# A decoder layer on one Trainium2 core: two weight matrices centred once, two of the four norms without a mean, every engine's order written anew

## What is computed

```python
def _layernorm(x, axis=-1, eps=1e-05):
    m = jnp.mean(x, axis=axis, keepdims=True)
    v = jnp.var(x, axis=axis, keepdims=True)
    return (x - m) / jnp.sqrt(v + eps)
...
x = _layernorm(x + _L0_attn_ref(x, Wq, bq, Wk, bk, Wv, bv, Wo, bo, gamma, beta))
x = _layernorm(x + _L0_xattn_ref(x, ctx_1024, Wq, Wk, Wv, Wo))     # ... return out @ Wo
x = _layernorm(x + _L0_ffn_ref(x, w_gate, w_up, w_down))           # ... fp4_linear(h, w_down)
```

## Time and profile before

| | us |
|---|---|
| time, median of 3 runs | 372.71 (372.67 to 373.03) |
| span of the profiled execution (first to last instruction) | 371.1 |
| PE busy (matmuls, ends modelled) | 349.7 (94%) |
| DVE busy | 308.7 (83%) |
| POOL busy | 269.0 (73%) |
| ACT busy | 253.6 (68%) |
| chain that ended last, share on PE | 70% |

### The profile page before, as it was taken

One profiled execution on the slowest core, in us unless ns is written; L12 is line 12 of the kernel. 1 busy time (PEld: TensorE's weight loads), 2 busy tenths in 40 slices (PEclk: granted clock), 3 DMA queues, 4 the chain that ended last, 5 costly groups with the idle time before them and its releaser, 6 DMA issues.

```text
span 371.1 us, 7329 instructions
## 1 busy us (share of the span) xinstructions
PE 349.7 (94%) x2147; PEld 267.9 (72%) x2147; DVE 308.7 (83%) x858; ACT 253.6 (68%) x533; POOL 269.0 (73%) x453
## 2 busy tenths in 40 slices
PE   8999989999998999999999999999999999998774
PEld 7788646675775868787678877786767787887653
DVE  3998557567689998869989779979998998999994
ACT  2957766577676677678688767878767666864553
POOL 4404459958988699969689895898988569784535
PEclk9999999999999999999999999999999999999999
DMA  8900100001000001000000000100000000000010
GB/s 248 305 2 16 30 1 16 14 16 29 15 17 14 17 0 44 28 18 16 29 14 17 14 1 17 31 0 0 17 15 2 15 2 1 15 16 14 3 30 28
DMA packets 13586, 10.44 MB, mean 28 GB/s; under 512 B 971, under 2 KB 12396, under 8 KB 13548
## 3 DMA queue, kind: packets, MB, share of 16 engines
q1 hardware_dynamic: 12540, 7.89, 7.1%
q10 hardware_dynamic: 1008, 2.10, 1.7%
HBM read 7.88 MB, written 2.10 MB: 27 GB/s over the span
## 4 chain that ended last, share of the span: by engine, by line
PE 70%; DVE 9%; POOL 8%; issue 6%; ACT 4%; DMA 1%; SPq 0%; POOLq 0%; DVEq 0%
PE A L2892 13%; PE S L2862 12%; PE TP L2852 7%; PE F L2916 6%; PE TP L2880 6%; PE A L2936 5%; PE S L2871 3%; PE A L2813 2%; PE TP L2791 2%; POOL pe L440 2%; PE F L2791 2%; PE S L2791 2%; PE TP L2925 2%; PE A L2826 2%; PE A L2821 1%
## 5 line engine op out<-in xcount | busy, mean ns | idle before, releaser
L440 POOL TENSOR_TENSOR pe<-pe,srec 128x1024 f32<-128x1024 f32 x32 | 60.9, 1904 | 9.2 <-DVE srec L1860 8.9
L2862 PE MATMUL S<-M,x1T 128*128 128x512 f32 x128 | 60.7, 597 | 1.5 <-ACT pe L1076 1.4
L2892 PEld LDWEIGHTS A<-wvoT,wqkT 128*128 128x128 f32 x480 | 56.4, 192 | 3.1 <-issue 1.8
L2892 PE MATMUL A<-wvoT,wqkT 128*128 128x128 f32 x480 | 58.0, 276 | 0.1
L434 POOL TENSOR_TENSOR fold<-pe 128x512 f32<-128x512 f32 x32 | 40.9, 1277 | 14.6 <-ACT pe L1076 14.4
L1843 DVE TENSOR_REDUCE smax<-S 128x16 fp32r<-128x1024 f32 x32 | 38.7, 1211 | 3.3 <-PE S L2862 3.1
L1076 ACT ACTIVATE pe<-S 128x1024 f32<-128x1024 f32 x32 | 32.6, 1019 | 10.6 <-PE S L2871 10.3
L1081 ACT ACTIVATE wqkT<-TP 128x1024 f32<-128x1024 f32 x32 | 32.6, 1018 | 4.3 <-PE TP L2880 4.1
L2862 PEld LDWEIGHTS S<-M,x1T 128*128 128x128 f32 x128 | 22.2, 190 | 18.3 <-issue 15.3
L2916 PE MATMUL F<-w_gu_r,GT 128*128 128x352 f32 x168 | 35.1, 344 | 0.1
L2880 PE MATMUL TP<-ident,pe 128*128 128x128 f32 x256 | 33.5, 274 | 1.6 <-POOL pe L440 0.9
(11 more groups left out here) (247 smaller groups left out, 888.2 us busy)
## 6 DMA issues: line engine op xcount, KB each, us to landing
xT<-in_x_t SPq DMA_DIRECT2D x16, 128.0 KB, 2.2
x_sb<-in_x SPq DMA_DIRECT2D x16, 128.0 KB, 2.2
out<-yf SPq DMA_DIRECT2D x15, 128.0 KB, 1.8
M<-in_fw SPq DMA_DIRECT2D x1, 560.0 KB, 11.0
wqkT<-in_wq_t ACTq DMA_DIRECT2D x2, 256.0 KB, 4.6
wqkT<-in_wk_t ACTq DMA_DIRECT2D x2, 256.0 KB, 6.1
ctx_f<-in_ctx_t ACTq DMA_DIRECT2D x2, 256.0 KB, 7.0
wvoT<-in_wv_t ACTq DMA_DIRECT2D x1, 512.0 KB, 9.4
```

What stands on the lines that cost most here:

```text
L440: ge.tensor_tensor(w, w, spread(srec[n % NFO][:, :], HX, R), ALU.mult).then_inc(pn_made, 1)
L2862: last = te.matmul(S[:, half * BANK:half * BANK + BANK], x1T[b % 2][:, t * P:t * P + P], M[:, b // BH, HC * half:HC * half + HC, b % BH * ...
L2892: last = te.matmul(part(A2, t), pT[n % 2][:, j, :], vo[b % 2][:, j, :], start=(j == 0 and b not in SUM_ON_PE), stop=(j == NJ - 1))
```

## The change

**Weights.** The output weights of cross attention, [1024, 128], are centred over their 128 output features when they have landed: `wo_sums` and `wo_means` on DVE, `wo_centred` (one subtraction over 128x1024) on POOL; `hw_product` waits for that. The FFN's down weights are centred by the matmul that transposes them, with `centre` = identity - 1/128 in the place of the identity. What the two projections add to the residual stream then has a mean of zero over the features; x1 and x2 are themselves outputs of norms.

**Norms.** "cross" and "ffn" lose BN_STATS and BN_AGGR on DVE and the mean and shift steps on POOL. ACT squares each tile with an accumulated sum (`squares`; the squares themselves go to x2 as scratch), POOL turns the sum into variance plus epsilon in one TENSOR_SCALAR (`square_eps`), `rstd_of` stays, and ACT scales without a bias. "attn" and "post" stay as they are.

```diff
+            def squares_of(n, b, t, done):
+                y, made = {"cross": (yx, yx_made), "ffn": (yf, yf_made)}[n]
+                act.wait_ge(made, done)
+                wait_free(act, veps_made[n], b - 1)
+                if n == "cross":
+                    wait_free(act, sq_made["ffn"], T * (b - 2))
+                sc.activation(x2[b % 3][:, NBX * t:NBX * t + NBX, 0:BLK], blocks(y[b % 2][:, t, :], NBX), ACT.Square,
+                              accum_out=sq[n][b % 2][:, t:t + 1]).then_inc(sq_made[n], 1)
+            def scaled_norm(n, b, t, done, dst, y):
+                act.wait_ge(rstd_made[n], done)
+                sc.activation(dst, y, ACT.Copy, scale=rstd[n][b % 2][:, t:t + 1]).then_inc(normed[n], 1)
...
+            def square_eps(n, b):
+                pool.wait_ge(sq_made[n], T * b + T)
+                wait_free(pool, rstd_made[n], b)
+                ge.tensor_scalar(veps[n][:, :], sq[n][b % 2][:, :], 1.0 / D, LN_EPS, ALU.mult, ALU.add).then_inc(veps_made[n], 1)
+            def wo_centred():
+                pool.wait_ge(wo_step, 2)
+                w = wvoT[:, 1, :, :]
+                ge.tensor_tensor(w, w, spread(wo_sum[:, :], NJ, P), ALU.subtract).then_inc(wo_made, 1)
...
+            def wo_sums():
+                dve.wait_ge(o_loaded, 16)
+                ve.tensor_reduce(wo_sum[:, :], wvoT[:, 1, :, :], AX.X, ALU.add).then_inc(wo_step, 1)
...
             def hw_product(half):
                 pe.wait_ge(v_loaded, 16)
-                pe.wait_ge(o_loaded, 16)
+                pe.wait_ge(wo_made, 1)
...
-                        last = te.transpose(F0[:, k * P:k * P + P], fw[:, 2 * NK * P + k0:2 * NK * P + k0 + P], ident[:, :])
+                        last = te.matmul(F0[:, k * P:k * P + P], fw[:, 2 * NK * P + k0:2 * NK * P + k0 + P], centre[:, :],
+                                         start=True, stop=True)
```

**Orders.** The lists of calls of all five engines are written anew; nearly every call has moved. Dead options (`SUM_ON_PE`, `WHOLE_GATE`, `TILE_SUM_ON_PE`, all empty or false before) are gone, and `keep_warm` in the last 40 us runs 24 transposes in six places where it ran 18 in two. Of the lists, two calls as the diff has them:

```diff
             pe.wait_ge(const_made, 5)
+            project_kv(0)
             g_product(0)
-            project_kv(0)
```

2972 lines of the change are left out of this document (1367 added, 1605 removed).

## The result

The changed kernel takes **379.10 us** (378.75 to 380.38, four runs), the kernel before 372.87 on the same chip: a ratio of 1.0175, 95% interval 1.0157 to 1.0193. It is 1.7% slower; I had said 369.9 and a range up to 378.

The account below looks back on a forecast made before the run. PE's matmuls, with holes, were taken as the bound, DVE at 330 to 360 us. 371.1 + 8.6 - 5.5 - 3.5 - 2.4 = 368.3 us of span, plus 1.6, gave 369.9; own range 365 to 371.9, wider 363 to 378.

Parts of the forecast that it names:

- start: Up to the first M: late xT, a longer chain behind the first projection and a slower clock cost 8.6 us.
- first softmax: PE's 3.5 us idle between first scores and transposed probabilities is covered by work moved there: -3.5 us.
- middle, 60 to 330: Engine load changes on the chain give 2.6 us and new orders 3: -5.5 us, ends 0 and -12.
- end: From 330 us, where DVE is the bound, three norms' statistics of 0.8 us each leave: -2.4 us, ends 0 and -4.
- Scaled by the loads: Middle: each engine's chain time times its load change, 33 x 0.09 + 30 x 0.047 - 15 x 0.12 = 2.6 us gained.
- 3 us for new orders: Middle: new orders close part of PE's 18 us of holes, between 0 and 10 us, taken as 3.
- The weights: Centring the output and FFN down weights costs nothing, unless the wait for the load blocks DVE.
- covered by the wait for xT: Start: DVE's waits for the FFN and output weights, and the reduces, are hidden by the wait for xT.
- The loads of the engines: Whole kernel: DVE's busy time 27.9 us lower, POOL's 12.6 (some 11 as a sign), ACT's 31 higher.
- ACT takes DVE's place: Rival: ACT's squares hold up PE, the middle gains nothing, 376.8 us; 0.33 together with a start not won back.
- a late start with no denser middle gives a slower kernel by my own terms: Sign of being wrong: late first projection without a denser middle means a slower kernel; slower had 0.33.

Follow-up runs that it names:

- b6_nostats: Kernel before, with the statistics and aggregates of the cross attention and FFN norms left out and nothing in their place: 372.18 us.
- a9_stats: Changed kernel with the old start and DVE's fw and wo steps later, plus dummy statistics and aggregates put back on DVE: 379.19 us, against 374.03 without them.
- b4_norm_nosq: Kernel before, old orders, with the new norms and centring, but ACT squaring one column of each tile, without sums of squares: 377.91 us.
- a4_warm: Changed kernel with 45 warm-up products on PE in place of 13: 378.12 us.
- a1_loads: Changed kernel with xT of sequence 0, the attention weights and kv's bias as SP's first three loads: 379.44 us.
- a8_nosq: Changed kernel with the old start and DVE's fw and wo steps later, ACT squaring one column per tile without sums: 373.15 us, against 374.03 with them.

## Why the prediction was wrong, point by point

The forecast's terms against PE's idle time and clock, as read in the section on the result:

| term | forecast, us | measured, us |
|---|---|---|
| start | +8.6 | +10.4 |
| first softmax | -3.5 | -2.1 |
| middle, 60 to 330 | -5.5 | -0.5 |
| end | -2.4 | -1.8 |
| sum | -2.8 | +6.0 by parts, +5.8 in the span |

**The middle: the step that failed.** I had -5.5 and it is -0.5, 5.0 of the 8.6 us by which the span was missed. "Scaled by the loads", 33 us of DVE on the chain times 9%, priced the statistics as if they stood on the chain in the measure of DVE's whole work. They hold 1.0 us of it, and b6_nostats, which took them all away, won 0.7 us in the whole kernel and 0.1 between the marks. PE waited for other results of DVE; the statistics lay between them in time that nobody waited for. The other half of the term, 3 us for new orders, had no row behind it. The new lists do use the freed room, since the same work put back, in a9_stats, costs them 5.2 us; but by PE's idle time they are no denser for it than 0.5 us, 2.2 won from 60 to 120 us and 1.7 lost from 120 to 330.

**The weights: a term put at nothing.** Centring wo costs 2.4 us ahead of the first mark in the old orders (b4_norm_nosq). In the changed kernel its price isn't measured by itself; it lies in the start.

**The start: right in its mechanism, short by 2.2 us at the first M.** I had +8.6 and the first M is 10.76 late. xT began its use at 15.39, 7.5 us later, where I had 6.3 with an end of 7.4: full DMA engines carried the sum, but 1.2 us are missing from it. The Trainium skill's "DMA: Bandwidth & Descriptors", section "Issuing engines are not separate DMA queues", by which ScalarE's 2048 KB count in full, agrees: SP's own 1810 KB would be 1.85 / 0.35 = 5.3 us. From there to the first M I had 4.6 + 1.0 us and it took 6.5: the lower clock took 2.0 and not 1.0. At the full clock, in a4_warm, the same chain took 4.48, so its 4.6 was right. That DVE's waits for fw and wo were "covered by the wait for xT" was right, and a1_loads showed that xT covered nothing but itself and them: I had named the wait for wo as the next to end, it was that for fw.

**The first softmax: right, with too large a hole.** The hole closed as forecast. It was 2.1 us of idle time in the window of 50 to 60 us, and I had made it 3.5 by pieces priced one by one.

**The end: near its size, for another reason.** PE's idle time behind 330 us fell by 3.2 us, of which the added `keep_warm` transposes take some 1.4. I had -2.4 because DVE was busy for 28.8 of 30 us. But without the statistics the old end takes 42.4 us in place of 42.9: a busy share of 96% was not a bound. What PE waits for there are single results of a serial chain, such as ScalarE's copy of the transposed h (0.99 us, twice). The gain comes from work that the new order has left for that stretch, so that I had it nearly right was luck. The new order also has longer waits there, 1.92 and 1.24 us.

**The loads of the engines.** DVE fell by 18 us, where I had 27.9: neighbours on DVE overlap (two BN_STATS of 0.29 and 0.28 us start 0.21 apart, at 49.02 and 49.23 in the timeline before), so durations summed one by one are more than they occupy. ACT rose by 10, where I had 31, and POOL fell by 7, where I had 11 to 12.6. The rows of the change, from the groups of its profile:

```profile
L991 ACT ACTIVATE x<-yx,rstd_cross 128x128 f32<-128x128 f32 x32 | 12.0, 393 | 1.8 <-POOL rstd_cross L464 1.1 <-POOL rstd_cross L502 0.4
...
L983 ACT ACTIVATE x<-yx 128x128 f32<-128x128 f32 x32 | 9.6, 303 | 0.8 <-DVE yx L1858 0.2
...
L983 ACT ACTIVATION_READ_ACCUMULATOR x<-yx 128x1 f32 x32 | 6.1, 192 | 0.0
```

A square with its sum is 303 and 192 ns, the 0.48 us forecast, but the next instruction starts 0.31 us behind the square (371.83 and 372.14 in the timeline of the last step); and the norm without a bias takes 393 ns for the 484 of the earlier trace rows, which I had not seen coming. All squares with their sums occupy 23.5 us of ScalarE, where their durations add up to 31.3.

**The rivals.** "ACT takes DVE's place" had the nearest time, 376.8, with a middle that gains nothing, and the wrong cause for it: a8_nosq gives ScalarE's sums 0.9 us at most. That its sum came within 2.3 us was in part luck, since a start too small by 1.8 stood against an end too small by 0.8. Its other ingredient, a start that is not won back, is what happened. I had the sentence "a late start with no denser middle gives a slower kernel by my own terms", and gave it, together with ACT, a third.

## What to carry to other kernels

An engine's busy share, or its share of the chain, doesn't price an operation: read the chain piece by piece and count the pieces of that operation. Here that gave 1.0 us, the share gave 3, and leaving the work out gave 0.7. Compare two kernels by a mark only where the same work stands on both sides of it; otherwise go by the idle time of the engine that bounds. In this kernel, whose PE was busy without gaps to speak of, time lost before the first product is lost in full, 8.33 us at 69 us and still 8.32 at 328, while work taken off an engine that isn't waited for gives next to nothing. When loads are reordered, follow every wait that stands behind the first one, on each engine, since one late load hides the next.
